# Neighbourhood attention in a vision tower: heads on 32 rows each, score products in pairs, and identity products in every tile and at the seam of the stage

## The reference

```python
xs = x @ fc1_w.T + fc1_b                      # 192 -> 96
a  = xs @ convA_w.T + convA_b                 # 96 -> 64
b  = a @ convB_w.T + convB_b                  # 64 -> 96
xs = gelu(b + xs)
# neighbourhood attention over the grid H x W = 64 x 37, 4 heads of 24 numbers, window 5 x 5
q, k, v = split(xs @ qkv_w.T + qkv_b)         # per head
logits  = (q * 24 ** -0.5) . k[window] + rpb[offset]
out     = softmax(logits over the 25) . v[window]
xs = (out @ proj_w.T + proj_b) @ fc2_w.T + fc2_b
return x + xs
```

## Time and profile before

| | us |
|---|---|
| median of 3 runs | 1039.59 |
| lowest, highest | 1038.16, 1042.99 |
| profiled execution | 1044.56 |
| its span | 1042.8 |
| PE busy in the span | 893.7 (86%) |
| PE weight loads | 627.3 (60%) |
| DVE busy | 522.7 (50%) |
| ACT busy, POOL busy | 312.0, 312.6 (30% each) |

### The profile page before, as it was taken

One profiled execution on the slowest core, in us unless ns is written; L12 is line 12 of the kernel. 1 busy time (PEld: TensorE's weight loads), 2 busy tenths in 40 slices (PEclk: granted clock), 3 DMA queues, 4 the chain that ended last, 5 costly groups with the idle time before them and its releaser, 6 DMA issues. The chain is left out here.

```text
span 1042.8 us, 18476 instructions
## 1 busy us (share of the span) xinstructions
PE 893.7 (86%) x6044; PEld 627.3 (60%) x6044; DVE 522.7 (50%) x1712; ACT 312.0 (30%) x860; POOL 312.6 (30%) x308
## 2 busy tenths in 40 slices
PE   6668999988999988987899799995772999999990
PEld 5557777756646655544565477774671666666660
DVE  5994788874853322222745378864674222222220
ACT  1333333322743322222123266662200222222210
POOL 3883000000000000000025145541007288888555
PEclk9999999989989999998998599996555999999995
DMA  8779000000008999994340000000205245555322
GB/s 259 221 251 421 19 0 0 0 1 0 2 7 325 423 423 422 423 423 158 98 167 0 1 2 1 0 2 1 72 0 137 62 97 101 100 103 99 44 23 23
DMA packets 64447, 127.98 MB, mean 123 GB/s; under 512 B 26910, under 2 KB 47184, under 8 KB 54912
## 3 DMA queue, kind: packets, MB, share of 16 engines
q1 hardware_dynamic: 34432, 117.79, 30.7%
q0 software_dynamic: 29952, 9.36, 6.7%
HBM read 114.93 MB, written 11.98 MB: 122 GB/s over the span
## 5 line engine op out<-in xcount | busy, mean ns | idle before, releaser
L1168 POOL MEMSET xg<- 96x74 f32 x1 | 0.2, 157 | 438.2 <-PE bank L1142 438.2
L1714 POOL DMA_INDIRECT out_dram<-yr,put x48 | 105.7, 2203 | 64.5 <-issue 42.6
L1700 POOL DMA_INDIRECT zr<-z_rows,take x48 | 66.5, 1386 | 85.3 <-issue 83.9
L1778 PE MATMUL bank<-zTa,w 128*128 128x372 f32 x256 | 89.6, 494 | 0.8 <-DVE zTb L1852 0.8
L1861 DVE TENSOR_TENSOR hT<-sg,bank 128x372 f32<-128x372 f32 x64 | 31.8, 539 | 106.9 <-ACT sg L1822 63.1
L1002 DVE COPY eh<-bank 128x384 f32<-128x384 f32 x32 | 17.8, 557 | 118.8 <-PE bank L1038 118.8
L1778 PEld LDWEIGHTS bank<-zTa,w 128*128 128x128 f32 x256 | 47.3, 193 | 38.1 <-ACT sg L1822 8.4
L1060 PE MATMUL bank<-w2s,eg 128*64 128x192 f32 x768 | 69.4, 330 | 0.0
L1792 PE MATMUL bank<-w2r,hT 128*124 128x192 f32 x384 | 66.1, 329 | 0.8 <-DVE hT L1861 0.8
L716 PE MATMUL bank<-wtok_g,xT 128*111 128x192 f32 x264 | 47.9, 332 | 20.9 <-DVE y L629 20.9
L1792 PEld LDWEIGHTS bank<-w2r,hT 128*124 128x124 f32 x384 | 61.9, 187 | 3.9 <-issue 3.9
(11 more groups left out here) (286 smaller groups left out, 1819.9 us busy)
## 6 DMA issues: line engine op xcount, KB each, us to landing
w1s<-in_w_dram SPq DMA_DIRECT2D x32, 1152.0 KB, 12.6
w2s<-in_w_dram SPq DMA_DIRECT2D x32, 1152.0 KB, 14.6
w<-in_w_dram SPq DMA_DIRECT2D x8, 1024.0 KB, 7.7
xt<-in_x_dram SPq DMA_DIRECT2D x22, 336.0 KB, 4.2
xT<-in_xT_dram SPq DMA_DIRECT2D x22, 333.0 KB, 3.5
ys<-eo SPq DMA_DIRECT2D x64, 48.0 KB, 10.0
w2r<-in_w2r_dram SPq DMA_DIRECT2D x8, 384.0 KB, 4.7
e<-ys SPq DMA_DIRECT2D x21, 96.0 KB, 2.0
```

Of the source, the lines that this page charges most:

```text
L1700: nc.gpsimd.indirect_dma_start(zr[b][:, j, :], None, z_rows, bass.IndirectOffsetOnAxis(ap=take[:, k:k + 1], axis=0), bounds_check=NROW - 1 ...
L1714: nc.gpsimd.indirect_dma_start(rows_out, bass.IndirectOffsetOnAxis(ap=put[:, k:k + 1], axis=0), yr[e % 2][:, j, :], None, bounds_check=OUT ...
L1778: nc.tensor.matmul(bank[to + 2 * part + half][:, 0:HS], w13[b][:, 0, at:at + 128], zTa[b][:, half * HS:(half + 1) * HS], start=True, stop= ...
```

## The change

Four things change, all in the near stage.

- **Rows.** The weights of query and key are padded to 32 columns a head, so queries, keys and `kT` have 128 rows. The score product of a head takes 32 rows of the query and the same 32 rows of `kT`. The spread goes; DVE adds the bias and multiplies by the constant in one `tensor_scalar` on 128 x 111 elements. The table `head` goes.
- **Waits.** The scores of two heads are issued right behind each other behind one wait: heads 0 and 1 for all logits of the tile before, heads 2 and 3 for the logits of heads 0 and 1.
- **Identity products.** `dense_near(3)` stands ahead of every `transpose_h`, `dense_near(4)` ahead of the keys of pairs 7 to 10, six products with `kT` ahead of the query of tiles 0, 1 and 2, and one ahead of the scores of heads 0 and 1 in each of the 22 tiles.
- **PE's loop.** The second half on PE is written out for all steps (`straight`); the other engines keep their loops.

```diff
+def straight(stages, n, buffers):
+    for s in range(n + max(lag for lag, _ in stages)):
+        for lag, step in stages:
+            if 0 <= s - lag < n:
+                step(s - lag, (s - lag) % buffers)
...
-        kT = sb("kT", [WN, XCOLS])
+        kT = sb("kT", [128, XCOLS])
...
-        qx = [sb(f"qx{b}", [WN, NHN, TP]) for b in range(2)]
+        qx = [sb(f"qx{b}", [128, TP]) for b in range(2)]
...
-                nc.vector.tensor_scalar(kT[:, bass.ds(PADR * S + p * PAIR, PAIR)], bank[4][0:WN, 0:PAIR], Cc["bk"], None, ALU.add).then_inc(s_fKc, 1)
+                nc.vector.tensor_scalar(kT[:, bass.ds(PADR * S + p * PAIR, PAIR)], bank[4][:, 0:PAIR], Cc["bk"], None, ALU.add).then_inc(s_fKc, 1)
...
-                nc.vector.scalar_tensor_tensor(out=qx[b][:], in0=bank[0][0:WN, 0:TP].unsqueeze(1).to_broadcast([WN, NHN, TP]), scalar=Cc["bq"], in1=Cc["head"].unsqueeze(2).to_broadcast([WN, NHN, TP]), op0=ALU.add, op1=ALU.mult).then_inc(s_nq, 1)
+                nc.vector.tensor_scalar(qx[b][:], bank[0][:, 0:TP], Cc["bq"], float(np.float32(DN ** -0.5)), ALU.add, ALU.mult).then_inc(s_nq, 1)
...
             def transpose_h(p, b):
-                if isinstance(p, int) and p < 6:
-                    dense_near(3)
+                dense_near(3)
...
             def keys(p, b):
+                if isinstance(p, int) and p >= T // 2 - 4:
+                    dense_near(4)
...
-                nc.tensor.matmul(bank[4][0:WN, 0:PAIR], Cc["wk"], xg[:, bass.ds(PADR * S + p * PAIR, PAIR)], start=True, stop=True).then_inc(s_fK, 1)
+                nc.tensor.matmul(bank[4][:, 0:PAIR], Cc["wk"], xg[:, bass.ds(PADR * S + p * PAIR, PAIR)], start=True, stop=True).then_inc(s_fK, 1)
...
             def query(t, q):
+                if isinstance(t, int) and t < 3:
+                    for _ in range(6):
+                        nc.tensor.matmul(bank[5][:, 0:256], ident, kT[:, 0:256], start=True, stop=True)
...
             def scores(t, q, heads):
-                first = (B - WIN + PADR) * S if isinstance(t, int) and t == T - 1 else t * TP
+                first = (B - WIN + PADR) * S if t == T - 1 else t * TP
                 pe.wait_ge(s_nq, t + 1)
+                if t or heads[0]:
+                    pe.wait_ge(s_nl, 4 * t + heads[0])
+                if heads[0] == 0:
+                    nc.tensor.matmul(bank[1][:, 0:256], ident, kT[:, 0:256], start=True, stop=True)
                 for head in heads:
-                    if after(t, 1) or head >= 2:
-                        pe.wait_ge(s_nl, 4 * t + head - 1)
-                    nc.tensor.matmul(bank[1 + head % 2][0:TP, 0:KW], qx[q % 2][:, head, :], kT[:, bass.ds(first, KW)], start=True, stop=True).then_inc(s_nS, 1)
+                    rows = slice(head * VW, (head + 1) * VW)
+                    nc.tensor.matmul(bank[1 + head % 2][0:TP, 0:KW], qx[q % 2][rows, :], kT[rows, first:first + KW], start=True, stop=True).then_inc(s_nS, 1)
...
-            over_tiles(pe, [(0, query), (3, values), (1, lambda t, q: scores(t, q, (0, 1))), (5, proj),
-                            (1, lambda t, q: scores(t, q, (2, 3))), (3, transpose_w), (5, fc2), (4, values_out)], T, unroll=4, tail=2)
+            straight([(0, query), (3, values), (1, lambda t, q: scores(t, q, (0, 1))), (5, proj),
+                      (1, lambda t, q: scores(t, q, (2, 3))), (3, transpose_w), (5, fc2), (4, values_out)], T, 4)
```

More of the change, by code:

```diff
@@ L61 @@
           ("phi", HALF, 2 * NE), ("scale", HALF, 1), ("image", TP, GB + 1), ("b1s", 128, NE * HB)]
-PACK_C = [("fc1", HALF, 2 * WN), ("conva", WN, CONV), ("convb", CONV, WN), ("wq", WN, WN), ("wk", WN, WN),
+PACK_C = [("fc1", HALF, 2 * WN), ("conva", WN, CONV), ("convb", CONV, WN), ("wq", WN, 128), ("wk", WN, 128),
           ("wv", WN, WN), ("proj", NHN * VW, WN), ("fc2", WN, ED), ("bv", TP, WN), ("bfc2", TP, ED),
-          ("bfc1", WN, 1), ("bconva", CONV, 1), ("bconvb", WN, 1), ("bq", WN, 1), ("bk", WN, 1), ("bproj", WN, 1),
-          ("head", WN, NHN), ("router", HALF, 2 * EX), ("before", TP, TP), ("count", TP, SP_), ("number", TP, T), ("spare", SP_, NST), ("real", TP, T),
+          ("bfc1", WN, 1), ("bconva", CONV, 1), ("bconvb", WN, 1), ("bq", 128, 1), ("bk", 128, 1), ("bproj", WN, 1),
+          ("router", HALF, 2 * EX), ("before", TP, TP), ("count", TP, SP_), ("number", TP, T), ("spare", SP_, NST), ("real", TP, T),
           ("gain", 128, 2 * EX)]
@@ L1429, in query @@
                     pe.wait_ge(s_fVc, 2)
-                nc.tensor.matmul(bank[0][0:WN, 0:TP], Cc["wq"], xg[:, bass.ds(PADR * S + t * TP, TP)], start=True, stop=True).then_inc(s_nQ, 1)
+                nc.tensor.matmul(bank[0][:, 0:TP], Cc["wq"], xg[:, bass.ds(PADR * S + t * TP, TP)], start=True, stop=True).then_inc(s_nQ, 1)
             def value(j, b):
@@ L1998, in lay_out @@
         "bfc1": col(f["L1_attn_fc1_b"]), "bconva": col(f["L1_attn_convA_b"]), "bconvb": col(f["L1_attn_convB_b"]),
-        "bq": col(bqkv[0:WN]), "bk": col(bqkv[WN:2 * WN]), "bproj": col(f["L1_attn_proj_b"]),
-        "head": (np.arange(WN)[:, None] // DN == np.arange(NHN)[None, :]).astype(np.float32) * np.float32(DN ** -0.5),
+        "bq": heads(bqkv[None, 0:WN]).T, "bk": heads(bqkv[None, WN:2 * WN]).T, "bproj": col(f["L1_attn_proj_b"]),
         "router": chunks(f["L1_ffn_gate_w"].T), "before": (w[:, None] < w[None, :]).astype(np.float32),
```

3 lines of the change are left out of this document (2 added, 1 removed).

## The result

| | before | after |
|---|---|---|
| median, us | 1039.59 | 1096.76 |
| lowest, highest | 1034.37, 1042.99 | 1080.87, 1119.65 |
| profiled execution, its span | 1044.56, 1042.8 | 1080.87, 1079.1 |

Ratio 1.0461, 95% interval 1.0402 to 1.0521 (it leaves out the two slowest of the five runs of the changed kernel; the quotient of the medians is 1.055). Forecast were 1060.6 us and a range to 1070; the result lies outside. The five runs of the changed kernel spread over 39 us, those of the kernel before over 9, and the mean granted clock goes with them: 0.912 for the run of 1080.87, 0.896 for the median, 0.873 for 1119.65.

A forecast was written before the change was run, and what follows sets the result against it. PE's order in a near tile bounds, with the DVE-ACT circle within 0.2 us. Terms 13.1 + 4.2 + 1.1 + 3.2 - 1.1 + 0.5 = +21.0 us on the median 1039.59 give 1060.6; 8-in-10 range 1047 to 1070.

The forecast's parts named there:

- I take the clock to hold: End of the dense layers: added identity products fill the idle stretch, so the clock stays full; this part sums to +4.2 us.
- the 23.2 us for tiles 3 to 6: Near stage, four tiles at the forecast full-clock 5.80 us each.
- the 17.0 for the first three: Near stage, first three tiles: 6.0, 5.5 and 5.5 us, 17.0 instead of 18.12 at half clock, -1.1 us.
- Rival C: Near tiles: PE's waits lose the clock, tiles about 9 us, 1130 in all, or a short fall costing 5 to 8; chance 0.08.
- Dense layers, their tail and the way to the first scores: Ahead of the tiles: added identity products at full clock cost +4.2, +1.1 and +3.2 us.
- The tile at full clock: Near stage, PE: 2.39 + 2.88 + 0.43 + 0.10 = 5.80 us instead of 5.07, over 18 tiles +13.1 us.
- T: Start of a tile's first pair of score products on PE, from which the forecast counts its times.
- The last pair: Behind tile 21: the last pair of heads is late by some 0.5 us, +0.5.
- A: Near tiles: DVE-ACT circle bounds, identity product fits into PE's waiting; tile 5.47 us, +12.9, 1052.5 in all; chance 0.13.
- the DVE-ACT circle: Near tile: DVE's logits, ACT's exponentials, DVE's reciprocal and next logits; 5.13 us before, 5.47 forecast after the change.
- B: Near tiles: array time counts, DVE's logits early enough; 0.02 us gained per tile, about 1041 in all; chance 0.07.
- The fourfold pace: Near-stage scores: by the skill, four heads cost 0.44 us of array time; 18 x 0.43 = 8 us better, 1033.

## Why the prediction was wrong

**The step that failed** is "I take the clock to hold", with the 23.2 us for tiles 3 to 6 and the 17.0 for the first three that rest on it. I had a row for it: 1.00 over 79 us with PE busy two thirds. From it I concluded that an engine busy for 5.2 of 5.8 us couldn't lose its clock. But the products of that stage are not passes on 32 rows, and the busy share treats a pass on 32 rows like one on 96. The runs showed that the clock doesn't hold: in tile 0 and tiles 2 to 6 it was at half for all or part of the time, and tiles 0 to 6 took 55.4 us instead of 40.2. And they showed that the passes aren't alike: 1054.72 and 1052.00 us on 96 rows with waits of 0.34 and 0.60, 1105.02 and 1146.34 us on 32; and with the identity products and the merged wait in both 1070.27 against 1092.24. The rows account for some 22 us of the loss; the first fall, in tile 1, comes on 96 rows too, and its cause is open.

Rival C had the lost clock, at 0.08, but for another reason and with the wrong size. It put the fall down to PE's waiting, and a wait of 0.60 us on 96 rows kept the clock. Its tile of 9 us was 10.00, and its 1130 is more than its terms give (1039.6 + 70 + 8.5 = 1118). Its two cases (5 to 8 us, or all tiles) left out what happened: a clock below full in six of the 22 tiles in one trace, in nine in the other, and by the times in more in other runs. For the profiled execution that is 15 us; for the median, 15.9 us above it, it would be 31 (the median is 36 above the forecast's 1060.6).

**Point by point, the rest of the sum.**
- Dense layers, their tail and the way to the first scores: forecast 4.2 + 1.1 + 3.2 = 8.5, measured 8.7. The run with these products alone gave 7.6 in its span, against 4.2 + 1.1 + 3.2 - 1.1 = 7.4; but the profiled run of before is 5 us above its median, and by the ratio of the runs (1.0092) the products cost 9.6.
- The tile at full clock: forecast 5.80, measured 5.85. Pair to pair 1.66 (1.70), first pair to transposes 2.29 (2.39), the rest 3.56 (3.41). DVE's first logits begin 0.73 behind T (0.75), its second maximum is there at 1.51 (1.55). The fourteen tiles from tile 7 on take 82.0 us, 0.8 more than 14 x 5.80.
- The query row on DVE: 0.33 where 0.25 was forecast from a row of 96 elements on 111 partitions; off the path, as said.
- The prediction's 694.74 for the first scores of tile 21 is 0.17 too late: in the trace they start at 694.57, so 18 tiles at 5.06.
- The last pair: +0.5 forecast, -0.6 measured, together with all that stands behind it.
- PE written out instead of looped: forecast 0; 1070.27 written out, 1069.16 in the loop, on different chips.

Had the clock held in tiles 0 to 6, the profiled run would have been 36.3 - 15.2 = 21.1 us longer than before, where 21.0 were forecast. That close a match is in part luck: single terms were off by 0.2 to 1.1 us and cancel, and the run of the kernel before that it is measured against is 5 us above the median. Against that median, 1080.87 - 15.2 is 26 us more. The sum was sound within some 5 us, and the condition on which all of it stood was not.

**The rivals.** A's place for the product is real: moved into the wait it makes the tile 5.30 at full clock, even under the 5.47 that I gave the DVE-ACT circle, which was too long by at least 0.17. But it isn't where the change puts it. B fell with the second pair's start, 1.66 us behind the first where it needed less than 1.3. The fourfold pace of the Trainium skill's "TensorEngine Tiling (Array Packing)", section Theoretical Speedup, wasn't tried: no run issued four heads side by side. In pairs, 0.89 went to 0.62, so 1.4 times and not 2, the changes of tiling included. The page's section PSUM Bottleneck again agrees with the trace: DVE's reading of the bank is what the second pair waits for, 0.61 us.

The second mistake is in the range. It had room for a fall of 5 to 8 us or of 70, each at 0.04, and for nothing between. A clock that falls in a stage of 22 like tiles can be gone for any number of them.

## What to carry to other kernels

Before TensorE's passes are put on fewer rows, see what DVE does per result: here the pairs saved 0.27 us of array time each, and the second pair waited 0.61 for DVE. Where a forecast rests on a full clock, look for a row with the same kind of pass at full clock; a busy share from other passes doesn't stand for it. And identity products paid a little where the engine idled at a seam (104.7 instead of 109.2 us for the tiles behind it, 0.35% of the whole by the ratio), while the one on the path of each tile cost 0.55 us.

## What the runs showed of the hardware

- TensorE may run at 1.2 GHz without one gap: 10.24 of 10.24 us busy, in 16 tiles running, on two chips.
- Passes on 32 rows hold the clock less than passes on 96 or 128 rows at the same places: 1146.34 against 1054.72 us; with identity products in both, 1092.24 against 1070.27; and with only one product of 256 columns changed, 1083.24 against 1066.39.
- They aren't needed for a fall: with all identity products and 96 rows the clock was at half for 10.24 us, and with a wait of 2.22 us it fell again and again (1129.78 us).
- Adding work can save the clock. 128 columns more in each tile made 1151.33 us into 1065.25 (at half for 3.4 us, not for 204.8); a product of 256 columns taken away made 1096.76 into 1110.97.
- Two copies of 111 x 192 elements on DVE, meant to bring a wait from 0.34 to about 1 us, took it to 2.22: they last 0.26 and 0.25 us with POOL idle and 1.37 and 0.64 with POOL at work. One statistics instruction of the same size lasts 0.35 to 0.36 either way, and took the wait to 0.60.
- Two row tiles side by side give 1.4 times the pace (0.62 for 0.89 us), by the distance to the next row.
